# Two half adds on GpSimd in place of one, for the last two adds of a quarter

## The reference

```
x = x + L0(groupnorm(x))     # sign, depthwise 3x3 of signs, PReLU, batch norm,
                             # sign, pointwise 64x64 of signs, PReLU, batch norm, + residual
x = x + L1(groupnorm(x))     # involution

def L1(x, W, b):             # x: (B, 64, 56, 56)
    filters = einsum('bchw,oc->bohw', x, W) + b     # 576 = 64 channels x 9 taps
    patches = the 9 shifted copies of x (3x3, zero padding)
    return sum over the 9 taps of patches * filters
```

## Time and profile before

| | before |
|---|---|
| median of 3 runs | 711.1 us (708.56 to 713.46) |
| profiled execution | 709.95 us, span 708.0 us |
| busy: DVE | 645.6 us, 91% of the span, 983 instructions |
| busy: PE | 616.0 us, 87%, 8017 |
| busy: POOL | 604.2 us, 85%, 264 |
| busy: ACT | 566.4 us, 80%, 837 |
| mean granted PE clock | 0.973 of full speed |

### The profile page before, as it was taken

How to read it: one execution, slowest core, us unless ns; L and a number is a source line. 1 busy time by engine, 2 the same in 40 slices (tenths; PEclk the granted TensorE clock), 3 DMA queues, 4 the chain that set the end, 5 groups by cost and what they waited for, 6 DMA issues and landing times.

```text
span 708.0 us, 18826 instructions
## 1 busy us (share of the span) xinstructions
PE 616.0 (87%) x8017; PEld 261.0 (37%) x8017; DVE 645.6 (91%) x983; ACT 566.4 (80%) x837; POOL 604.2 (85%) x264
## 2 busy tenths in 40 slices
PE   2539789999899989999898989999998999898897
PEld 1314344343434334343433334343434344341333
DVE  4739889999999999999899989999999999999796
ACT  6976998989989888989889878998989898846010
POOL 2001677999999999999899998999999999999896
PEclk9859999999999999999999999999999999999899
DMA  5226879899999999999999999999999998989884
GB/s 205 89 55 156 156 153 237 184 261 230 260 231 213 239 213 264 215 256 230 255 211 217 242 212 247 206 260 231 249 231 207 254 209 186 205 193 212 188 170 134
DMA packets 34280, 148.13 MB, mean 209 GB/s; under 512 B 3348, under 2 KB 11540, under 8 KB 32276
## 3 DMA queue, kind: packets, MB, share of 16 engines
q0 software_dynamic: 17232, 81.89, 61.8%
q1 hardware_dynamic: 16940, 65.03, 27.4%
q10 hardware_dynamic: 24, 0.00, 0.0%
HBM read 26.03 MB, written 25.69 MB: 73 GB/s over the span
## 4 chain that ended last, share of the span: by engine, by line
POOL 59%; DMA 14%; ACT 8%; DVE 6%; PE 6%; issue 5%; SPq 1%; POOLq 0%; ACTq 0%; DVEq 0%
POOL prod L410 25%; DMA prod<-prod 12%; POOL ob L442 11%; POOL prod L431 9%; POOL prod L380 5%; POOL prod L407 5%; DVE prod L984 5%; POOL prod L424 3%; PE tap_ps L516 3%; ACT unused L619 2%; ACT ab L619 2%; DMA mirror<-q 1%; ACT st L619 1%; PE tap_ps L538 1%; DMA xb<-in_x_dram 1%
## 5 line engine op out<-in xcount | busy, mean ns | idle before, releaser
L984 DVE SCALAR_TENSOR_TENSOR prod<-tap_ps,bias,q 128x784 f32<-128x784 f32 x508 | 498.8, 1025 | 32.2 <-PE tap_ps L516 24.6
L516 PE MATMUL tap_ps<-q,w_t 64*64 64x392 f32 x2304 | 473.7, 507 | 45.5 <-DMA mirror<-q 25.6
L516 PE MATMUL tap_ps<-mirror,w_t 64*64 64x392 f32 x2304 | 467.9, 507 | 0.0
L516 PEld LDWEIGHTS tap_ps<-q,w_t 64*64 64x64 f32 x2304 | 152.8, 134 | 245.3 <-DVE prod L984 173.7
L410 POOL TENSOR_TENSOR prod<-prod 128x2352 f32<-128x2352 f32 x45 | 240.1, 5336 | 0.5 <-DMA prod<-prod 0.5
L559 PE MATMUL tap_ps<-signs,dw_diag 64*64 64x392 bf16 x2304 | 137.0, 342 | 6.5 <-DVE dw_diag L884 2.0
L516 PEld LDWEIGHTS tap_ps<-mirror,w_t 64*64 64x64 f32 x2304 | 138.7, 134 | 0.2 <-issue 0.2
L619 ACT ACTIVATE ab<-tap_ps,col 128x784 bf16<-128x784 f32 x128 | 120.3, 992 | 20.1 <-PE tap_ps L559 20.1
L442 POOL TENSOR_TENSOR ob<-prod 128x784 f32<-128x784 f32 x63 | 124.7, 1979 | 6.5
L619 ACT ACTIVATE st<-st 128x1 f32<-128x1 f32 x368 | 88.4, 251 | 32.4 <-DVE st L960 11.6
L559 PEld LDWEIGHTS tap_ps<-signs,dw_diag 64*64 64x64 bf16 x2304 | 71.9, 110 | 100.0 <-issue 56.0
(11 more groups left out here) (120 smaller groups left out, 339.3 us busy)
## 6 DMA issues: line engine op xcount, KB each, us to landing
prod<-prod POOLq DMA_DIRECT2D x48, 1176.0 KB, 10.8
out_dram<-ob SPq DMA_DIRECT2D x31, 784.0 KB, 7.5
xb<-in_x_dram SPq DMA_DIRECT2D x15, 1568.0 KB, 13.3
prod<-prod POOLq DMA_DIRECT2D x15, 1568.0 KB, 13.1
mirror<-q SPq DMA_DIRECT2D x64, 203.0 KB, 4.8
xb<-in_x_dram SPq DMA_DIRECT2D x2, 784.0 KB, 5.6
out_dram<-ob SPq DMA_DIRECT2D x2, 392.0 KB, 2.3
prod<-in_L_conv_W_dram SPq DMA_DIRECT2D x1, 288.0 KB
```

What stands on the lines that cost most here:

```text
L516: mm = pe.matmul(rows3(tap_ps[to, slot, side, 0:CH]), w_t[own, k, :], moving, start=True, stop=True)
L984: v.scalar_tensor_tensor(place.rearrange("p j (a b) -> p j a b", b=WD), psum.rearrange("p j (a b) -> p j a b", b=WD), s_(t, B4) if k == 4 ...
```

## The change

The front add and the result add of a quarter are each split into two adds of half the pixels, 392 (`CH`). A result half waits for the front half of the same pixels. `summed` and `summed35` count two per quarter, and the waits on them are doubled. The form of a quarter called paired, which no quarter used (`PAIRED` was empty), is taken out.

```diff
             def add35(t, qq):
                 g = quarter(t, qq)
                 pr = planes(g)
+                if not on_pool(g):
+                    return
+                pool.wait_ge(summed_wide, g + 1)
                 if in_fours(g):
-                    pool.wait_ge(summed_wide, g + 1)
                     pool.wait_ge(mean_added, with_mean(g))
-                    pool.tensor_tensor(pr[4], pr[4], pr[8], ALU.add).then_inc(summed35, 1)
...
-                elif on_pool(g):
-                    pool.wait_ge(summed_wide, g + 1)
-                    pool.tensor_tensor(pr[3], pr[3], pr[5], ALU.add).then_inc(summed35, 1)
+                    into, more = pr[4], pr[8]
+                else:
+                    into, more = pr[3], pr[5]
+                for a, b in zip(halves(into), halves(more)):
+                    pool.tensor_tensor(a, a, b, ALU.add).then_inc(summed35, 1)

             def final(t, qq):
...
-                if on_pool(g):
-                    pool.wait_ge(summed35, pooled(g))
-                else:
+                if not on_pool(g):
                     pool.wait_ge(summed_wide, g + 1)
-                pool.tensor_tensor(ob[:, qq, :], pr[5] if in_fours(g) else pr[3], pr[4], ALU.add).then_inc(summed, 1)
+                for half, (result, a, b) in enumerate(zip(halves(ob[:, qq, :]), halves(pr[5] if in_fours(g) else pr[3]), halves(pr[4]))):
+                    if on_pool(g):
+                        pool.wait_ge(summed35, 2 * pooled(g) - 1 + half)
+                    pool.tensor_tensor(result, a, b, ALU.add).then_inc(summed, 1)
...
+            def halves(ap):
+                return ap[:, 0:CH], ap[:, CH:QP]
...
-                    sp.wait_ge(summed, quarter(t, qq) + 1)           # store, on SP
+                    sp.wait_ge(summed, 2 * quarter(t, qq) + 2)
...
-                    wait(dve, summed, g - BUFS + 1)                  # product, k == 3, on DVE
+                    wait(dve, summed, 2 * (g - BUFS + 1))
```

More of the change, by code:

```diff
@@ L203, in in_fours @@
             return on_pool(g) and g % QUARTERS in FOURS
[L205 to L211, removed]
         def in_banks(g):
@@ L392, in add_early @@
                 pr = planes(g)
-                if in_pairs(g):
-                    pool.wait_ge(prod_done, KK * g + 8)
-                    pool.tensor_tensor(pr[6], pr[6], pr[7], ALU.add).then_inc(summed67, 1)
                 if is_kept(g):
@@ L407, in add_wide @@
                     pool.tensor_tensor(pr[:, 4:6, :], pr[:, 4:6, :], pr[:, 6:8, :], ALU.add).then_inc(summed_wide, 1)
-                elif on_pool(g) and not in_pairs(g):
+                elif on_pool(g):
                     pool.wait_ge(mean_added, with_mean(g))
@@ L414, in add_wide @@
                     else:
-                        pool.wait_ge(summed67, paired_early(g))
+                        pool.wait_ge(summed67, kept(g))
                     pool.tensor_tensor(pr[:, 3:5, :], pr[:, 3:5, :], pr[:, 5:7, :], ALU.add).then_inc(summed_wide, 1)
+            def halves(ap):
+                return ap[:, 0:CH], ap[:, CH:QP]
             def add35(t, qq):
@@ L420, in add35 @@
                 pr = planes(g)
+                if not on_pool(g):
+                    return
+                pool.wait_ge(summed_wide, g + 1)
                 if in_fours(g):
-                    pool.wait_ge(summed_wide, g + 1)
                     pool.wait_ge(mean_added, with_mean(g))
-                    pool.tensor_tensor(pr[4], pr[4], pr[8], ALU.add).then_inc(summed35, 1)
-                elif in_pairs(g):
-                    pool.wait_ge(summed_wide, g + 1)
-                    pool.wait_ge(mean_added, with_mean(g))
-                    pool.tensor_tensor(pr[3], pr[3], pr[8], ALU.add).then_inc(summed35, 1)
-                elif on_pool(g):
-                    pool.wait_ge(summed_wide, g + 1)
-                    pool.tensor_tensor(pr[3], pr[3], pr[5], ALU.add).then_inc(summed35, 1)
+                    into, more = pr[4], pr[8]
[3 more added lines that the diff above has]
+                    pool.tensor_tensor(a, a, b, ALU.add).then_inc(summed35, 1)
             def final(t, qq):
@@ L1158 @@
 FOURS = 0,
-PAIRED = ()
 FOLD_FOUR_DELAY = 6
```

## The result

Over 20 runs of each the changed kernel takes 713.69 us in the median (708.67 to 718.41), the one before 711.25 (705.25 to 715.91). The ratio is 1.0041, with a 95% interval of 1.0021 to 1.0061: 2.9 us slower, between 1.5 and 4.3. The forecast was 715 us, a loss of 4.3.

What follows compares the result with a forecast made beforehand. POOL and DVE, waiting on each other, were taken as the bound. 0.50 us per tile over twelve tiles, 6.0, less 0.8 and 1.2, plus 0.2 and 0.1, gave +4.3 on 711.1: 715 us, range 707 to 721.

Steps and rivals of the forecast that it cites:

- Price of one more instruction: Fixed cost on POOL of each additional add: 0.13 us, bounds 0.11 and 0.17.
- The tail rows: Four adds running into one another at POOL's end: 1.80 us for 784 elements, 3.48 for 1568, so 0.12 fixed.
- The third pair of rows: Wide add's 5.17 us against 3.48 for 1568 elements: 1.69 per 784 and 0.11 fixed.
- A quarter with the fold in front: Three of four quarters on POOL: fold end to result end from 3.90 to 3.96 us, +0.08 used.
- the gap: 0.14 us in which POOL waits for its own front add before the result add; claimed to go with halves.
- A tile of POOL: POOL's added work over the four quarters of one tile: +0.50 us, 6.0 us over twelve tiles.
- Leg A: POOL alone, from L387's start to the result add that releases DVE: 13.3 us, growing by 0.21 to 13.5.
- What of it shows: Of 6.0 us, off 0.8 at L407's wait and 1.2 where DVE's path decides; on 0.2 and 0.1: +4.3 us.
- PE's stall at the mirrors: PE's wait for mirror transfers, 1.26 us at 338.07; changes to mirror timing were costed at nothing.
- Halves that run free: Rival: a second half costs only its elements, 0.84 us; -4.0 us over twelve tiles, 707 us; chance 0.16.
- Halves as dear as an add that waited: Rival: each half costs 0.22 us more and POOL's 0.14 wait stays; +16, 727 us; chance 0.17.
- The clock: Rival: shifted POOL work removes two half-speed PE stretches, some 2 us each, or adds one, +2; chance in favour 0.09.

Runs made afterwards that it cites:

- both4: Front and result add each in four pieces of 196, each result piece waiting for its own front piece, against the kernel before: 1.0349, +24.8 us.
- wait_both: Both adds in halves, but the first result half waits for both front halves, against the kernel before: 1.0104, +7.4 us.
- front4: Front add in four pieces of 196, result add whole, against the kernel before: 1.0164, +11.6 us.
- result4: Result add in four pieces of 196, front add whole, against the kernel before: 1.0162, +11.5 us.

## Why the prediction was right

- **Price of one more instruction**, 0.13, bounds 0.11 and 0.17: measured 0.14 with halves and 0.147 with quarters of an add. The tail rows were the right ones to take it from; independent adds end to end behave as the halves do. (The third pair of rows gives 0.10 and not 0.11: 5.17 less three times 1.69. It changes nothing.) The estimate by the Trainium skill's "GPSIMD Engine Reference", section Instruction dispatch (tens of cycles for the dispatcher's call, 0.04 us at 50) does not agree as the price of one more add: the 0.147 us of `both4` is three to four times as long. What the section says of a core starting the next instruction early does agree: result halves begin while front halves are still recorded.
- **A quarter with the fold in front**, 3.96 us from fold end to result end: measured 3.96. That the gap goes was shown by keeping it (`wait_both`, 4.17).
- **A tile of POOL**, +0.50: measured +0.42 between the two tiles shown (39.13 and 39.55), and 0.52 by the parts, 0.08 three times and 0.14 twice. Leg A, 13.5 us by the forecast, is 13.45 (232.43 to 245.88).
- **What of it shows.** The forecast was 6.0 us less 2.0, plus 0.3; the runs say 2.9, with 4.3 at the edge of the interval. If the split is 6.5 us of POOL, some 3.6 are hidden (2.2 to 5.0 by the interval), more than the 2.0 forecast. That is a subtraction: the one traced execution of the changed kernel hides nothing. Where waits are seen to shrink they shrink by more than the forecast took off: 3.9 us with the mirrors sooner, 5.2 with DVE let go earlier. The term that was too small is what a wait can hide. The forecast took at most one tile's growth of a leg off each, 0.21 or 0.29 us; but with the mirrors sooner two waits of L387, 2.2 us together, vanish whole, so the growth of several tiles must have gone into one wait, as far as one execution of each kernel shows. And I had PE's stall at the mirrors inside DVE's path as a constant; it gives way. PE's waits there grow when DVE is let go earlier (25.6 to 33.5 us) and fall when POOL has more to do: 25.6 before, 23.9, 21.0, 16.7 and 16.8 in `wait_both`, `front4`, `result4` and `both4`. Which of the two hid the 3.6 us is open.
- **The rivals.** Halves that run free: out, by `both4`. Halves as dear as an add that waited, 0.22: out, by the price. The clock: the change left it as it was, with 0.975 in the median after and 0.973 to 0.975 before, and two low stretches in either trace, so nothing speaks for this rival here. Its mechanism is real for larger additions: no low stretch falls between 130 and 650 us in the traces of `wait_both`, `front4`, `result4` and `both4`, and their median clocks are 0.977 to 0.980 where the kernel before has 0.973 beside them. The waits at the mirrors named there were worth 5 us when shortened; they belonged into the sum and not beside it. That they limit how much of POOL's time shows is not shown.

## What to carry to other kernels

Splitting a pair of adds to hide the wait between them loses when it needs two more instructions of 0.14 us each and hiding the wait wins 0.21: +0.07 us where the gap exists, and all of the 0.28 in the quarter of the cases that had none. When several loops are within a few tenths of a microsecond per tile of each other, freeing one engine moves its wait to the next loop: look for where the freed engine would stand next, and shorten that one as well. What an engine that is nearly the bound still waits in the steady part is the most that more work on it can hide, 9.1 us here; of what `both4` adds beyond that, nearly all shows.

## What was not expected of the hardware

- An earlier release of DVE, with the same instructions, made the kernel slower by 0.45%, with PE idle for 3.02 us at one mirror and a mean clock of 0.65 behind it; with the mirrors sooner the same release cost nothing.
- Cutting the first mirror's transfers of 203 KB into two of 101.5 KB brought quarter 0 in some 0.8 us sooner (4.8 and 5.4 us to 4.0 and 4.6), though the DMA engines are 0.99 busy from 130 to 650 us, and the whole mattered by 0.7%.
- A wait of PE of 2.60 us was followed by the full clock in one kernel, a wait of 1.26 us by a low stretch in another.
- One constant, which quarters use the four-plane fold, made 13%: the mirrors took 9.4 us to land in place of 4.8, and why is open.
